# One branch for the whole kernel, slice weights folded in the front, and slices that begin inside the last superblock of the first sum

## The reference

```
1  graph convolution:  agg = A_norm (z @ W);  relu(agg + b)
2  slice attention:    w   = softmax(((z @ W_x + b_x) @ W_slice + b_slice) / temperature), 8 heads of 64
                       tok = (z @ W_fx + b_fx)^T w / sum(w);  q, k, v, softmax, out_slice;  out = out_slice w^T @ W_out
3  hypergraph:         two times A^T A (h @ W), PReLU, with the input added
4  experts:            top 2 of 8 experts, gelu(z @ W1 + b1) @ W2 + b2, weighted
```

## Time and profile before

| | us |
|---|---|
| median of 3 runs | 1292.38 (1290.71 to 1295.51) |
| the profiled execution | 1290.6 |
| its span | 1288.9 |
| PE busy | 1218.0 (95%) |
| DVE busy | 577.5 (45%) |
| ACT busy | 483.3 (37%) |
| POOL busy | 200.1 (16%) |

### The profile page before, as it was taken

The page is one execution under the profiler, slowest core; times in us unless marked ns, Lnnn a source line. Parts: engine busy times, 40 slices in busy tenths (PEclk is TensorE's granted clock), DMA queues, the critical chain, the costliest instruction groups (busy, mean ns, idle before and its releaser), DMA issues.

```text
span 1288.9 us, 20242 instructions
## 1 busy us (share of the span) xinstructions
PE 1218.0 (95%) x7462; PEld 841.7 (65%) x7462; DVE 577.5 (45%) x1595; ACT 483.3 (37%) x1189; POOL 200.1 (16%) x205
## 2 busy tenths in 40 slices
PE   3699999899999999999999999999999998989996
PEld 2477777745558544457777644457777777778885
DVE  5977877557755412222333322322224747223221
ACT  5876666277733787840000001100222352212221
POOL 3000000023310000000000000000000233577764
PEclk7699999999999999999999999999999989999998
DMA  6133113400004155566555455578856666556663
GB/s 192 30 129 129 68 62 129 170 5 0 1 1 131 48 157 154 153 153 128 128 128 132 150 153 153 151 168 180 161 128 159 188 190 175 136 130 150 151 146 66
DMA packets 256969, 159.98 MB, mean 124 GB/s; under 512 B 172832, under 2 KB 243951, under 8 KB 256732
## 3 DMA queue, kind: packets, MB, share of 16 engines
q1 hardware_dynamic: 245788, 143.58, 40.5%
q0 software_dynamic: 11072, 14.97, 6.6%
HBM read 82.15 MB, written 36.35 MB: 92 GB/s over the span
## 4 chain that ended last, share of the span: by engine, by line
PE 62%; DMA 3%; DVE 3%; issue 1%; POOL 1%; POOLq 0%; ACT 0%; ACTq 0%; DVEq 0%; SPq 0%
PE bank L1036 21%; PE bank L1022 21%; PE bank L2521 7%; PE bank L2386 6%; PE bank L1057 2%; PE bank L1675 2%; DMA out<-weights,first_places 2%; PE bank L1927 1%; PE bank L2374 1%; DMA weights<-in_L_ffn_W 1%; PE bank L1917 0%; DVE bnbuf L835 0%; DVE weights L2078 0%; DVE tb L2043 0%; DMA normed<-rows_and_gates,agg_in_out 0%
## 5 line engine op out<-in xcount | busy, mean ns | idle before, releaser
L1036 PE MATMUL bank<-weights 128*128 128x512 f16 x1250 | 270.7, 379 | 1.3 <-issue 1.3
L1022 PE MATMUL bank<-weights,agg_in_out 128*128 128x320 f16 (+1 forms) x2000 | 268.6, 296 | 0.0
L1022 PEld LDWEIGHTS bank<-weights,agg_in_out 128*128 128x128 f16 x2000 | 195.7, 98 | 70.4
L1036 PEld LDWEIGHTS bank<-weights 128*128 128x128 f16 x1250 | 122.0, 98 | 149.2 <-issue 2.1
L1163 PE MATMUL bank<-weights,agg_in_out 128*128 128x320 f16 (+1 forms) x1000 | 160.4, 298 | 2.8 <-DVE agg_in_out L643 1.1
L851 POOL TENSOR_TENSOR shift<-shift,rstd 128x5 f32<-128x5 f32 x15 | 3.7, 245 | 852.0 <-ACT rstd L856 852.0
L543 ACT CAST weights<-bank 128x500 f16<-128x500 f32 x157 | 110.5, 723 | 61.6 <-PE bank L532 61.5
L2354 ACT ACTIVATE weights<-bank,weights 128x128 f32<-128x128 f32 (+1 forms) x156 | 56.0, 411 | 167.8 <-PE bank L2386 145.3
L2521 PE MATMUL bank<-weights 128*128 x448 | 110.3, 393 | 2.8 <-ACT weights L2354 2.6
L1163 PEld LDWEIGHTS bank<-weights,agg_in_out 128*128 128x128 f16 x1000 | 92.1, 98 | 28.6 <-issue 2.1
L2386 PE MATMUL bank<-wk,weights 128*128 128x128 f32 (+1 forms) x624 | 107.3, 327 | 3.1 <-DMA weights<-in_L_ffn_W 2.5
(11 more groups left out here) (428 smaller groups left out, 1460.5 us busy)
## 6 DMA issues: line engine op xcount, KB each, us to landing
weights<-counts_source_target SPq DMA_DIRECT2D x50, 800.0 KB, 4.6
counts_source_target<-weights SPq DMA_DIRECT2D x5, 4000.0 KB, 13.9
weights<-in_L_ffn_W SPq DMA_DIRECT2D x39, 512.0 KB
weights<-in_L_ffn_W SPq DMA_DIRECT2D x4, 1024.0 KB, 5.8
residual<-in_x SPq DMA_DIRECT2D x4, 640.0 KB, 5.1
rows_and_gates<-normed SPq DMA_DIRECT2D x1, 1980.0 KB, 8.6
out<-residual SPq DMA_DIRECT2D x1, 1792.0 KB
first_rows_and_gates<-normed SPq DMA_DIRECT2D x1, 1320.0 KB, 7.2
```

The source lines that it names most:

```text
L1022: last = nc.tensor.matmul(bank, source[:, 5 * k + c, part * F + fh * P:part * F + fh * P + P], MB[:, k, c, h * HALF:h * HALF + w], start=( ...
L1036: last = nc.tensor.matmul(ps[j][:, :], MB[:, k, c, j * P:(j + 1) * P], source[:, 5 * k + c, :], start=(k == 0 and c == 0), stop=(k == 4 an ...
```

## The change

1. **One block, one branch.** The second block is gone. Each engine branches once, and both paths are written out to the end: front, `If` fast path (sum, slices, attention, way back, step 3, experts), `Else` the same for the general path. Functions that were local to the second block are moved out whole (`turn`, `hidden`, `take` are now `tile_turn`, `tile_hidden`, `tile_take`). What was the meeting of the engines is two waits of PE ahead of the way back, on the copies of the attention.
2. **Folding in the front.** The folded weights have a place of their own. SP loads W_x, W_slice (two) and b_x ahead of the packed keys, temperature and b_slice behind them; only group 0 of x is loaded early, groups 1 to 4 behind the keys. POOL spreads the bias columns ahead of its gathers. The PE instructions of the folding stand ahead of the keys' transposes and between quads 8 and 9 (in place of five idle products); the scaling of the weights on DVE is at slot 26 of superblock 0.
3. **Slices inside the last superblock.** Turns and logits of chunks 0 and 1, and the turn of chunk 2, stand between the quarter parts. The last five graph products and rows stand in slice rounds 2 to 6, and the last group's statistics, roots and normalising in rounds 6 to 12. Tokens have one bank (5), the product one (6), weights are turned in banks 0 and 1, the slices are summed in 4 and 7. The 14 idle products are gone.
4. Statistics and normalising of superblocks 1 to 4 come up to eight slots earlier; POOL's adding starts with a copy in place of a cleared buffer and clears others after round 3.

```diff
@@ tensor engine, front
+            fold_turn_pe(pe)      # 8 transposes, waits for W_x
+            fold_bias_pe(pe)      # 4 products, waits for b_x, W_slice, POOL's copy and w_pos
             for b in range(NSB):
                 keys_turn_pe(pe, b)
@@ keys_turn_pe
+            if b < 2:
+                pe.wait_ge(fo_cp.sem, b + 1)
+                pe.wait_ge(fo_in.sem, b)
@@ vector engine, front
-            nc.vector.tensor_scalar(first, startf, ...).then_inc(w_pos.sem, 1)
+            nc.vector.tensor_scalar(first_edge, startf, ...).then_inc(w_pos.sem, 1)
+            fold_bias_dve(dve, step)   # 2 small, 2 of 128x512
             row_statistics_dve(dve, step, 2)
@@ GpSimd, front
+            pool.wait_ge(fo_ld.sem, 16 * 3)
+            pool.tensor_copy(colb, bcol ... to [P, NPAIR, P]).then_inc(fo_pr.sem, 1)
             pool.wait_ge(st.sem, 48)
             pool.wait_ge(w_pos.sem, 1)
@@ scalar engine, front: behind the squares of group 0
+                if k == 0:
+                    fold_copy_act(act)     # 2 copies of 128x512
@@ tensor engine, first sum
                     for q in range(AHEAD):
                         quad_pe(pe, q)
                         if q == 8:
-                            idle_products(0, 5)
+                            fold_pe(pe)            # 8 products
...
-                            if b == NSB - 1 and s == 18:
+                            if b == NSB - 1 and s == 14:
                                 pe.wait_ge(q_ev.sem, q_ev.at(QUADS))
                                 bound_pe(pe)
-                            if b == NSB - 1 and s == 19:
-                                fold_turn_pe(pe)
-                            if b == NSB - 1 and s == 28:
-                                fold_pe(pe)
+                            if b == NSB - 1 and s == 15:
+                                pe.wait_ge(p_out.sem, p_out.at(NC - 5))
+                            if b == NSB - 1 and s in (15, 17, 23):
+                                token_turn_pe(pe, (15, 17, 23).index(s))
+                            if b == NSB - 1 and s in (19, 21):
+                                logits_pe(pe, (s - 19) // 2)
...
-                    for n in range(NC - 5, NC):
-                        first_product_pe(pe, n)
-                with pe.Else():
-                    ...
-                slices_pe(pe)
-                attention_pe(pe)
+                    for n in range(2, NC):
+                        logits_pe(pe, n)
+                        if n + 1 < NC:
+                            token_turn_pe(pe, n + 1)
+                        if n < 7:
+                            first_product_pe(pe, NC - 7 + n)
+                        ...
+                        gather_slices_pe(pe, n - 2)
+                    gather_slices_pe(pe, NC - 2)
+                    gather_slices_pe(pe, NC - 1)
+                    attention_pe(pe)
+                    back_pe(pe)            # waits s_cd 8 and s_ca 8
+                    second_pe(pe)
+                    experts_pe(pe)
+                with pe.Else():
+                    ...
@@ vector engine, last superblock and slices
+                            if b == NSB - 1 and s in (22, 24):
+                                scores_dve(dve, step, (s - 22) // 2)
+                            if b == NSB - 1 and s == 27:
+                                weights_dve(dve, step, 0)
+                    quarter_copy(dve, nc.vector.tensor_copy, NSB - 1, 3, c_cd)
+                    for n in range(2, NC):
+                        scores_dve(dve, step, n)
+                        weights_dve(dve, step, n - 1)
+                        if n < 7:
+                            first_row_dve(dve, step, NC - 7 + n)
+                        if n == 6:
+                            statistics_dve(step, l2_st, NSB - 1)
@@ scalar engine, slices
+                    for n in range(2, NC):
+                        if n + 1 < NC:
+                            tokens_act(act, n + 1)
+                        keep_act(act, n - 2)
+                        exps_act(act, n)
+                        if n == 7:
+                            root_act(act, l2_st, l2_rt, NSB - 1)
+                        if 8 <= n < 13:
+                            ...
+                            normalise_row(NC - 5 + n - 8, l2_z)
```

More of the change, by code:

```diff
@@ new lines, in fold_copy_act, with fold_bias_pe @@
+        def fold_copy_act(act):
+            act.wait_ge(fo_tr.sem, 1)
+            for m in range(2):
+                nc.scalar.copy(wxT[:, 2 * m:2 * m + 2, :], ps[5 + m][:, :].rearrange("p (t f) -> p t f", t=2)
+                               ).then_inc(fo_cp.sem, 1)
+        def fold_bias_pe(pe):
+            pe.wait_ge(fo_ld.sem, 16 * 3)
+            pe.wait_ge(fo_pr.sem, 1)
+            pe.wait_ge(w_pos.sem, 1)
+            for t in range(NPAIR):
+                last = nc.tensor.matmul(ps[3][:, t * P:(t + 1) * P], colb[:, t, :], pair0, start=True, stop=True)
+            last.then_inc(fo_mm.sem, 1)
@@ L762, in front_sp @@
                          ).then_inc(st.sem, 16)
+            sp.dma_start(wx, w_x.rearrange("(k p) n -> p k n", p=P)).then_inc(fo_wx.sem, 16)
+            for h in range(2):
+                sp.dma_start(pair0[h * 64:h * 64 + 64, h * 64:h * 64 + 64], w_slice).then_inc(fo_ld.sem, 16)
+            with nc.allow_non_contiguous_dma(reason="a bias as columns, once"):
+                sp.dma_start(bcol, b_x.rearrange("(t p) -> p t", p=P)).then_inc(fo_ld.sem, 16)
             sp.wait_ge(y_ready.sem, 3)
@@ new lines, in slices_dve, with exps_act @@
+        def slices_dve(dve, step):
+            scores_dve(dve, step, 0)
+            for n in range(1, NC):
+                scores_dve(dve, step, n)
+                weights_dve(dve, step, n - 1)
+            weights_dve(dve, step, NC - 1)
+        def exps_act(act, n):
+            act.wait_ge(g_x.sem, g_x.at(n + 1))
+            for h in range(H):
+                last = nc.scalar.activation(ring[n % 4][:, h * G:(h + 1) * G], ring[n % 4][:, h * G:(h + 1) * G],
+                                            ACT.Exp, bias=sm[:, n % 2, h:h + 1])
+            last.then_inc(g_ex.sem, 1)
@@ new lines, in gather_slices_pe @@
+        def gather_slices_pe(pe, n):
+            w = ring[n % 4]
+            pe.wait_ge(g_w.sem, g_w.at(n + 1))
+            if n >= 2:
+                pe.wait_ge(w_cp.sem, w_cp.at(n - 1))
+            for t in range(NPAIR):
+                last = nc.tensor.transpose(ps[n % 2][:, t * P:(t + 1) * P], w[:, t * P:(t + 1) * P], ident[:])
+            last.then_inc(w_tr.sem, 1)
+            for k in range(KF):
+                last = nc.tensor.matmul(ps[ACC[k]][:, :], Z[:, n, k * P:(k + 1) * P], w,
+                                        start=(n == 0), stop=(n == NC - 1))
+            last.then_inc(w_ac.sem, 1)
@@ new lines, in tile_hidden @@
+        def tile_hidden(pe, n):
+            b, w = n % 2, parts(n) * P
+            pe.wait_ge(w_ld[b].sem, 16 * (n // 2 + 1))
+            pe.wait_ge(x_cp.sem, n + 1)
+            for m in range(KH):
+                if n >= 2 and m % 2 == 0:
+                    pe.wait_ge(h_ac.sem, 2 * (n - 2) + m // 2 + 1)
+                for k in range(KF):
+                    last = nc.tensor.matmul(ps[2 + 2 * b + m // 2][:, (m % 2) * w:(m % 2 + 1) * w],
+                                            w1b[:, b, k, m * P:(m + 1) * P], xT[:, b, k * w:(k + 1) * w],
+                                            start=(k == 0), stop=(k == KF - 1))
+                if m % 2:
+                    last.then_inc(h_mm.sem, 1)
@@ L2254, in _ @@
[L2254 to L2262 removed]
+                    dve.wait_ge(gd_z.sem, NC)
+                    general_sum_dve(dve, step, 0, 0, 1, from_z(dinv))
```

1800 lines of the change are left out of this document (917 added, 883 removed).

## The result

| | before | after |
|---|---|---|
| median of 6 runs each, us | 1295.76 (1290.71 to 1297.66) | 1280.8 (1276.2 to 1285.02) |
| ratio | | 0.990, 95% interval 0.988 to 0.993 |
| the profiled execution | 1290.6 | 1284.8 |
| its span | 1288.9 | 1283.0 |
| PE / DVE / ACT / POOL busy | 1218.0 / 577.5 / 483.3 / 200.1 | 1215.5 / 580.3 / 484.5 / 199.9 |

Forecast were 1279 us, a range of 1274.5 to 1285, and faster with a chance of 0.91. The median lies 1.8 us above the forecast. The interval of the ratio leaves out 1, so the kernel is faster, by 1%.

A forecast was written before the change was run, and what follows sets the result against it. PE was taken as the bound in the last superblock and the slices. Terms 14.1 + 0.4 + 0.8 + 0.1 - 0.5 - 2.5 = 12.4 us off 1290.6 gave 1278.2, 1280.0 against the runs' median; forecast 1279, range 1274.5 to 1285.

The forecast's parts named there:

- Stretch of sum and slices: Last superblock to end of slices, as PE's work: from 156.06 to 141.97 us, a gain of 14.1.
- slot 15: In the last superblock, a new PE wait for DVE's first operation on row 19: 0.25 us, ends 0 and 1.3.
- DVE 2.96 + 1.30 with some gaps, about 4.5: hidden, by 0.4: Slice rounds 2 to 6: DVE's work with the added row stays hidden behind PE's 4.96 us a round.
- The table switches and normalisings on ACT: Slice loop: ACT falls 1.5 to 2 us behind, recovers by round 12; cost 0, without cover 2.56.
- Where the blocks met: Attention to way back: PE waits for the copies alone, 0.85 us instead of 1.28; gain 0.4.
- The second flag reading, 0.8, and DVE's late start, 0.1: Past the blocks' meeting: PE's second flag reading and jump go, gain 0.8; DVE's rows start sooner, gain 0.1.
- The front: Ahead of the first quad: more bytes beside the gathers delay the second; cost 0.5, ends -0.5 and 1.8.
- The end jump: At the close, SP jumps over the general path after the last scatter; cost 2.5 us, from PE's 2.55.
- Rival A: At the close or DVE's start: the end jump is free, or DVE's early start helps; 1276 us, chance 19%.
- B: Slice loop: ACT or DVE late in two or three rounds, or a front at its 1.8 end; 1283 us, 13%.
- C: Slice loop bound by ACT's token copy, 1.38 us lost in every round; slower, 1299 us, chance 4%.
- D: Last superblock: slot 15 holds PE until the sum's work is out, first 8 us lost; 1287 us, chance 4%.

The follow-up runs named there:

- late_slices: Changed kernel with turns, logits, scores and exponentials of chunks 0 to 2 behind the sum instead of inside the last superblock; 1282.47 us, ratio 0.992.
- pool_narrow: Changed kernel with POOL adding only 8 of the 512 columns of the slice weights for chunks 1 to 6; one run, 1286.8 us.
- late_work: Changed kernel with DVE's row ahead of its round's weights, last group's statistics and roots one round later, ACT's first row counts earlier; 1276.4 us, ratio 0.988.
- as_else: Changed kernel with the general path as the If and the fast path as the Else; 1283.33 us, ratio 0.993.
- again: The changed kernel measured and profiled once more, unedited; 1279.68 us, ratio 0.991.
- act_load: Changed kernel with ACT copying the turned weights once more in slice rounds 11 to 16, twice more in 17 to 22; one run, 1279.5 us.
- count_early: Changed kernel with ACT counting step 3's first block of rows ahead of the last group's roots and normalising; one run, 1276.2 us.
- row_first: Changed kernel with DVE doing the graph product's row ahead of the round's weights in slice rounds 2 to 6; 1278.1 us, ratio 0.989.

## Why the prediction was right, step by step

Right in time, direction and mechanism. By steps, first the sum's term, then what was measured:

- **Stretch of sum and slices, 14.1.** The same stretch in after is 213.09 (the fifth product is 1.09 us later there) to 356.55, 143.46 us: 12.6. Of these, 3.6 are the folding, 2.5 the head start (late_slices), and the other 6.5 the gap, with its serial tail now inside the rounds. The missing 1.5 are the waits of 1.27 and 0.18 and the 0.09 by which slot 15 took more than 0.25. The step that failed is "DVE 2.96 + 1.30 with some gaps, about 4.5: hidden, by 0.4": the round was 5.21 us, the bound by 0.25, since the 1.30 were read from rows with POOL at rest. Five rounds of it, plus the statistics, are the wait.
- **The table switches and normalisings on ACT, 0.** At most the 0.18. In pool_narrow and late_work, where DVE isn't late, PE doesn't wait there at all, though the switches are in the loop, so that wait took both. Two loads of 1.28 us stand at 283.13 and 285.40, with the next operation 0.01 to 0.02 us behind each (284.43, 286.69), so the 4.5 us behind and the stalls of 2 to 3 us that the prediction works out from 2.66 us a switch don't come. Its reading of the earlier trace rows was wrong, too: no wait follows the load there.

```profile
265.97 2.02 ACT L1250 ACTIVATE wk<-wk,small 128x64 f32<-128x64 f32 x8
```

- **Where the blocks met, 0.4.** 0.5: 19.42 to 18.92 us from attention to way back at the same clock. In the first profile of after a lower clock (0.92) hid it and took 1.2 us more.
- **The second flag reading, 0.8, and DVE's late start, 0.1.** 1.2 up to step 3 (45.45 to 44.26), then 1.0 back in its first sum. This step failed: it didn't ask what is late next, and ACT's counts were. Net 0.2.
- **The front, -0.5.** -0.9 to -1.2, inside its bounds. The direction is as reasoned, more bytes beside the gathers; the first was issued 0.69 us earlier (18.00) and landed 0.64 later, and DVE passes that on, with 0.19 more for its second key.
- **The end jump, -2.5.** -0.7 (8.39 and 8.32 against 7.66 us from scatter to end), by as_else -0.95. The step that failed is the price: PE's 2.55 was the wrong neighbour for a jump of SP at the close, and "closing 2 to 3 us longer" didn't come. How long SP's jump itself takes stays open: SP's last wait, for PE, is 4.7 us before, 4.4 in as_else and 3.0 in after and again, so a part of the jump may lie beside the closing. The Trainium skill (Runtime: NRT & Kernel Launch, "Instruction fetch mechanics") has such a jump force a fetch, and these rows agree that it isn't free: from under 1 us to 3.5, by engine and place.

12.6 + 0.5 + 0.2 - 1.1 - 0.7 = 11.5 us, where 12.4 were forecast. Two stretches that the sum left out differ between profiles by more than most of these terms: ranks to experts (43.5 us before, 42.9 in again, 42.4 to 44.2 in all) and experts to scatter (246.6 to 256.8). The medians differ by 15.0 in the first comparison and by 12.3 in the second (1291.99 to 1279.68). The errors of the terms, -1.5, -0.7 and -0.6 on one side and +1.8 on the other, nearly cancelled, so the forecast's nearness is partly luck.

Rival A (a cheap end jump) was half true: the jump was 1.8 us cheaper than taken, and losses elsewhere took it. B named ACT or DVE; the lateness was there, but DVE's, through POOL. C and D are excluded, C by act_load, D by the 0.34 at slot 15.

## What to carry to other kernels

Work that is moved beside another engine must be priced from rows where that engine is also busy: the same addition was 0.42 us with POOL at rest and 1.20 beside it. When a wait is taken away, follow each engine to its next meeting, since 1.0 of 1.2 us came back 28 us later and one block of counts moved up won 1.8. Of the 12.6 us, merging the serial tail into the loop gave 6.5, moving work to where PE waits for others gave 3.6, and starting the loop early only 2.5. Idle products in a gap that stays can be worth keeping, as here.

## What was unexpected of the hardware

- PE after 3.8 us without work began the logits at half clock and paid 1.8 us for four products; with products on zeros in the gap the clock fell as well, but was back at 1.00 from 262.15 on.
- The same attention, with the same waits of PE inside, ran at 1.00 throughout in again, late_slices, count_early and late_work. In after and row_first it had 0.50 for some 4 us from 14 us into it on, a mean of 0.92, and took 1.7 us longer. No run shows what decides.
- A jump over the general path: 3.5 us on DVE ahead of its first quad, 0.7 to 0.95 us more at the close.
